# Attention scores on TensorE: four 32-row tiles in two rounds, or four 64-row tiles in one

## What is computed

```
Q = (q @ wq + bq).reshape(b, sq, H, DK).transpose(0, 2, 1, 3)
K = (k @ wk + bk).reshape(b, sk, H, DK).transpose(0, 2, 1, 3)
V = (v @ wv + bv).reshape(b, sk, H, DK).transpose(0, 2, 1, 3)
scores = jnp.einsum('bhqd,bhkd->bhqk', Q, K) / np.float32(np.sqrt(DK))
scores = jnp.where(mask[:, None, :, :] == 0, jnp.float32(-1e+20), scores)
A = jax.nn.softmax(scores, axis=-1)
out = jnp.einsum('bhqk,bhkd->bhqd', A, V).transpose(0, 2, 1, 3).reshape(b, sq, D)
out = out @ wo + bo
```

## Time and profile before

| | |
|---|---|
| median of 3 runs | 714.12 us (712.08 to 714.96) |
| the profiled execution | 715.84 us |
| its span in the profile | 714.0 us |
| busy: PE, DVE, ACT, POOL | 660.5, 510.5, 455.2, 320.0 us |
| PE L570 (scores), L607 (transposes) | 125.2, 120.3 us |
| DVE L1106 (maximum), L1122, L1065 | 108.9, 108.3, 91.8 us |
| POOL L500 (masked keys) | 95.5 us in 96 instructions |

### The profile page before, as it was taken

The page is one execution under the profiler, slowest core; times in us unless marked ns, Lnnn a source line. Parts: engine busy times, 40 slices in busy tenths (PEclk is TensorE's granted clock), DMA queues, the critical chain, the costliest instruction groups (busy, mean ns, idle before and its releaser), DMA issues.

```text
span 714.0 us, 26835 instructions
## 1 busy us (share of the span) xinstructions
PE 660.5 (92%) x9470; PEld 468.4 (66%) x9470; DVE 510.5 (71%) x1259; ACT 455.2 (64%) x1274; POOL 320.0 (45%) x540
## 2 busy tenths in 40 slices
PE   1999999999999999999999849899997899999995
PEld 1566666677777766666666536799993556666773
DVE  0599899878788778888888743344433788988884
ACT  1366777677777787777777533455524667777874
POOL 2244444467666653333377564255433345442110
PEclk9999999999999999999999769999995899999998
DMA  8333343322332310101011000122232000000100
GB/s 268 104 93 88 85 94 79 73 64 50 78 96 84 104 54 25 29 24 32 24 43 37 25 31 31 50 67 64 68 90 81 24 25 23 22 17 17 36 28 27
DMA packets 48527, 42.07 MB, mean 59 GB/s; under 512 B 6553, under 2 KB 42909, under 8 KB 47280
## 3 DMA queue, kind: packets, MB, share of 16 engines
q1 hardware_dynamic: 41632, 23.33, 11.6%
q10 hardware_dynamic: 4528, 13.25, 7.5%
q0 software_dynamic: 2272, 4.24, 1.9%
HBM read 25.41 MB, written 14.79 MB: 56 GB/s over the span
## 4 chain that ended last, share of the span: by engine, by line
PE 71%; issue 14%; POOL 7%; DVE 3%; ACT 2%; ACTq 1%; DMA 0%; SPq 0%; POOLq 0%; DVEq 0%
PE ps L570 11%; PE ps L607 10%; PE ps L738 5%; PE ps L811 5%; PE ps L800 5%; PE ps L663 5%; PE ps L644 4%; PE ps L680 4%; PE ps L746 4%; PE ps L719 3%; POOL k_by_j L500 3%; PE ps L664 2%; PE ps L766 2%; PE ps L592 2%; PE ps L691 2%
## 5 line engine op out<-in xcount | busy, mean ns | idle before, releaser
L1106 DVE TENSOR_REDUCE top<-ps 128x16 f32<-128x1024 f32 (+1 forms) x96 | 108.9, 1134 | 41.9 <-PE ps L570 40.2
L492 POOL TENSOR_TENSOR rstd<-spread,half_neg 128x1 f32<-128x1 f32 x80 | 44.5, 557 | 194.4 <-DVE spread L1199 115.2
L500 POOL TENSOR_TENSOR k_by_j<-k_t,cst 128x512 f32<-128x512 f32 (+1 forms) x96 | 95.5, 995 | 74.2 <-ACT k_t L915 37.8
L570 PE MATMUL ps<-k_by_j,q_t 32*64 32x256 f32 (+1 forms) x1536 | 125.2, 396 | 1.1
L607 PE MATMUL ps<-cst,prob 128*128 128x128 f32 x704 | 120.3, 291 | 1.1 <-ACT prob L936 1.0
L607 PEld LDWEIGHTS ps<-cst,prob 128*128 128x128 f32 x704 | 77.2, 144 | 62.0 <-issue 45.6
L1065 DVE RECIPROCAL inv<-ps 128x128 f32<-128x128 f32 x96 | 91.8, 956 | 32.3 <-PE ps L746 30.0
L1122 DVE TENSOR_TENSOR prob<-ps,top 128x1024 f32<-128x1024 f32 (+1 forms) x96 | 108.3, 1128 | 0.7
L936 ACT ACTIVATE prob<-prob 128x1024 f32<-128x1024 f32 (+1 forms) x96 | 94.8, 987 | 22.0 <-DVE prob L1122 21.7
L885 ACT ACTIVATE prob_t<-ps 128x512 f32<-128x512 f32 (+1 forms) x96 | 53.9, 561 | 38.7 <-PE ps L607 38.3
L873 ACT ACTIVATE prob_t<-ps 128x512 f32<-128x512 f32 (+1 forms) x96 | 53.9, 561 | 29.6 <-PE ps L607 28.5
(11 more groups left out here) (155 smaller groups left out, 1202.4 us busy)
## 6 DMA issues: line engine op xcount, KB each, us to landing
sorted_rows<-zero_rows ACTq DMA_DIRECT2D x32, 276.2 KB, 2.7
stage_m<-in_m SPq DMA_DIRECT2D x80, 64.0 KB, 1.9
mow<-in_mow SPq DMA_DIRECT2D x18, 256.0 KB, 3.0
stage_kv<-in_ctx_t SPq DMA_DIRECT2D x64, 64.0 KB, 1.7
rows_in<-sorted_rows SPq DMA_DIRECT2D x39, 65.0 KB, 1.8
wat<-in_wat ACTq DMA_DIRECT2D x1, 1280.0 KB, 6.5
x_t<-in_x_t SPq DMA_DIRECT2D x16, 64.0 KB, 1.9
stage_kv<-in_x_t SPq DMA_DIRECT2D x16, 64.0 KB, 1.7
```

Of the source, the lines that this page charges most:

```text
L500: pool.tensor_tensor(k_by_j[:, p, 0:nj, :], k_t[:, p:p + 1, :].broadcast_to([128, nj, TOK]), cst[:, cj:cj + nj].unsqueeze(2).broadcast_to( ...
L570: mm = pe.matmul(ps[S * b:S * b + S, 2 * p + bank, r * nj * S:(r + 1) * nj * S].rearrange("p (h k) -> p h k", k=S), q_t[rows_g, p, S * b:S ...
L1106: dve.tensor_reduce(top[:, p, 0:nh].rearrange("p (b h) -> p b h", b=2), sc, AX.X, ALU.max).then_inc(top_d, 1)
```

## The change

The scores of a pair are made in one round of four products. Each takes 64 partitions (half of the heads) and 512 columns, as a tile of 64 rows and 64 columns. For that the masked keys have 8 copies (4 with 8 heads), so L500 writes 1024 elements per partition in place of 512 (512 in place of 256 with 8 heads), and the columns of constants are wider. The semaphore between the rounds is gone, all eight transposes (four with 8 heads) stand together, and in the loops the four waits for a pair's scores stand in the slot before, between the products with the values and those of the row sums.

```
     def score_ready(pr):
         wait_pair(pe, pt1_e, pr, 2)
         if MASKED[pr.phase]:
             wait_pair(pe, mask_d, pr)
         wait_pair(pe, q_e, pr)
         wait_pair(pe, kj_d, pr)

     def score(pr):
-        p, nj = pr.p, heads(pr) // 4
+        p, nj = pr.p, heads(pr) // 2
         masked = MASKED[pr.phase]
         for bank in range(2):
-            rows_g = slice(32 * (2 * bank + r), 32 * (2 * bank + r) + 32)
+            rows_h = slice(S * bank, S * bank + S)
             for b in range(2):
                 mm = pe.matmul(
-                    ps[S * b:S * b + S, 2 * p + bank, r * nj * S:(r + 1) * nj * S].rearrange("p (h k) -> p h k", k=S),
-                    q_t[rows_g, p, S * b:S * b + S], k_by_j[rows_g, p, 0:nj, S * b:S * b + S],
-                    start=not masked and r == 0, stop=True, skip_group_check=True)
+                    ps[S * b:S * b + S, 2 * p + bank, 0:nj * S].rearrange("p (h k) -> p h k", k=S),
+                    q_t[rows_h, p, S * b:S * b + S], k_by_j[rows_h, p, 0:nj, S * b:S * b + S],
+                    start=not masked, stop=True, skip_group_check=True)
+        mm.then_inc(score_d, 1)
...
-        k_by_j = sb("k_by_j", [128, 2, 4, TOK])
+        k_by_j = sb("k_by_j", [128, 2, 8, TOK])
...
-                    p, nj = pr.p, heads(pr) // 4
-                    cj = C_J16 if nj == 4 else C_J8
+                    p, nj = pr.p, heads(pr) // 2
+                    cj = C_J16 if nj == 8 else C_J8
...
-                        scored = at(OFF_SCORE)
-                        if half == 0 and scored is not None:
-                            score_round(scored, 1).then_inc(score_d, 1)
...
+                    following = at(OFF_V)
+                    if following is not None:
+                        score_ready(following)
                     for k in range(step):
                         for g in range(4):
```

More of the change, by code:

```diff
@@ L69 @@
 BIASED = {0: 0, 1: 1, 4: 2}
-C_ID, C_J16, C_J8, C_IOTA, C_BASE = 0, 128, 132, 134, 142
-C_STEP, C_UPTO, C_BLOCK = 150, 166, 230
+C_ID, C_J16, C_J8, C_IOTA, C_BASE = 0, 128, 136, 140, 148
+C_STEP, C_UPTO, C_BLOCK = 156, 172, 236
 C_O16 = C_BLOCK + JB
@@ L264, in build @@
         neg_d, mask_d = sem("neg_d"), sem("mask_d")
-        round_d = sem("round_d")
         kj_d, rstd_d, gsc_d, res_d = (sem(k) for k in ("kj_d", "rstd_d", "gsc_d", "res_d"))
@@ L579, in slot @@
                 if pr is not None:
-                    p = pr.p
-                    wait_pair(pe, pt1_e, pr, 2)
-                    if MASKED[pr.phase]:
-                        wait_pair(pe, mask_d, pr)
-                    wait_pair(pe, q_e, pr)
-                    wait_pair(pe, kj_d, pr)
-                    score_round(pr, 0).then_inc(round_d, 1)
+                    if isinstance(pr.n, int):
+                        score_ready(pr)
+                    score(pr)
                 pr = follows(at, OFF_FY, FF)
@@ L665, in slot @@
                         .then_inc(proj_d, 1)
-                pr = at(OFF_SCORE)
-                if pr is not None and at(OFF_PV) is None:
-                    score_round(pr, 1).then_inc(score_d, 1)
                 pr = at(OFF_OUT)
@@ L1310, in constants @@
     cst[:, C_ID:C_ID + 128] = np.eye(128)
-    cst[:, C_J16:C_J16 + 4] = r[:, None] % 32 // 8 == np.arange(4)
-    cst[:, C_J8:C_J8 + 2] = r[:, None] % 32 // 16 == np.arange(2)
+    cst[:, C_J16:C_J16 + 8] = r[:, None] % S // 8 == np.arange(8)
+    cst[:, C_J8:C_J8 + 4] = r[:, None] % S // 16 == np.arange(4)
     cst[:, C_IOTA:C_IOTA + E] = np.arange(E)
```

11 lines of the change are left out of this document (7 added, 4 removed).

## The result

| | median of the runs, us | range | ratio to before [95% interval] |
|---|---|---|---|
| before | 714.54 | 712.08 to 716.69 | |
| after | 725.43 | 723.18 to 726.63 | 1.0158 [1.0122, 1.0194] |

The changed kernel is slower by 10.9 us; 726.0 was predicted. Its profiled execution is the fastest of its runs, 723.18 us, with a span of 721.4 (before: 715.84 and 714.0), so the two traces differ by only 7.4 us.

What follows compares the result with a forecast made beforehand. PE was taken as the bound (71% of the span), with a POOL–VectorE loop 0.17 us behind. LayerNorm +16.2, feed-forward +8.5, RMS -3.5, last phase -3.7, fills -3.5, router and combination -2.0 gave +12.0: 726 us, range 715 to 737.

Steps and rivals of the forecast that it cites:

- The round: Scores on PE: one round of 512 columns takes 1.01 us to the transposes; PE gains 0.25 us per 16-head slot.
- the keys' length: Masked keys on POOL (L500): 1024 elements take 1.89 us, 0.85 more than now.
- the hold: LayerNorm slots: normed on VectorE can't run beside POOL's masked keys and ends 0.08 us behind them.
- This ring: LayerNorm slots: POOL and VectorE wait on each other; the loop grows from 5.13 to 5.98 us, costing +16.2 us.
- Rival B: Masked keys on POOL cost twice the present, 2.08 us: +7.6 us, 733.7 us in all; chance 0.14.
- Rival A: VectorE gets in at a break within the longer keys instruction, so normed stays short: 704.4 us, faster; chance 0.09.
- Feed-forward slots: 15 periods with the feed-forward behind them: mean 7.9 us, 118.5 us in all against 110.08, +8.5 us.
- PE's own need, 110.08/15 - 0.25 = 7.1 us, is hidden below that: Feed-forward slots: PE needs only 7.1 us per slot, less than the 7.9 us mean set by POOL and VectorE.
- the ring over POOL: Feed-forward slots: power, longer keys, second power, then n_f take 2.95 us (before 2.28); whole slot 8.0 us.
- RMS slots: 14 slots without normed on VectorE: the longer keys fit POOL's idle time, PE's full 0.25 us each counts, -3.5 us.
- Last phase: Final stretch, 16 scores: PE is the bound and VectorE has no normed, so PE's gain counts, -3.7 us.
- Fills, router, experts: Two pipeline fills: -1.5 and -2 us from earlier scores; ten router and four combination slots: -2 us, bounds -4 and +2.

Runs made afterwards that it cites:

- The fastest kernel: Changed kernel with masked keys ahead of POOL's power where a LayerNorm follows, and the feed-forward score round between the transpose halves, against the kernel before: 696.79 us, 0.9729.

## Why the prediction was right, and where it was not

**The round, the keys' length and the hold** were right to a few hundredths: 1.02 us to the transposes (1.01 predicted), 1.90 us for 1024 elements (1.89), normed ending 0.08 us behind the keys, a period of 5.97 us (5.98), +11.3 and +5.0 us (+11.2, +5.0). This ring carries the result, and the kernel with y in PSUM shows that it is the reading of y from SBUF which holds normed. Under 1 us of the +11.3 is the clock: one of the 18 slots took 7.28 us at a mean clock of 0.77 in the first profile, and 6.21 at 0.90 in the second. Rival B's 2.08 us for the keys didn't come; nor did the estimate of 2.15 us from the Trainium skill's cycles per element (GPSIMD Engine Reference, Elementwise, side-by-side cycle accounting), against 1.90 in the trace. Rival A had assumed a break within an instruction. No run shows one. Between two instructions normed got in, and picked did not. The prediction put the 0.17 us that a round costs beside its columns down to a drain of TensorE; the measured 1.02 us fits a part that is paid once per round, but no run shows that it is a drain.

**Feed-forward slots**: the size was nearly right, +9.5 for +8.5, and the cause only half. The step "PE's own need, 110.08/15 - 0.25 = 7.1 us, is hidden below that" failed. PE's work is about that, but without its second round PE has to wait for xn_f, and the slot is 7.69 us even with short keys. Over the 15 slots the single round alone costs 3.7 us (113.8 in the kernel with short keys), long keys alone 8.5 us (118.6 in the kernel before with long keys), and both 9.5, since they lie side by side. The last two sums hold one slot of 10.1 us each. The prediction named "PE idle 0.8 us there ahead of xn_f's transpose" as a sign of the ring over POOL. It was there (0.78 us), and was no such sign: 0.69 of it stays when the keys are short. That one slot took 10.08 us instead of about 7.8, with a long wait and then half of the clock for a part of it, which no step had foreseen (below). Without it the 15 slots come to about +7.2, so that the size was so nearly right is in part luck.

**RMS slots**: -2.4 us for -3.5. The mis-sized term is PE's gain per slot. On its own stretch, first score to normed's transpose, it was even more than 0.25 us: 1.94 in place of 2.27 us. But the period shrank only from 5.21 to 5.01, because from normed's transpose to PE's output product (L674) it is now 1.31 us, 0.11 more than before. What L674 has to wait for, x_t on ScalarE, stands behind the two prob_t copies, and the first of these starts 1.77 us after the slot's first score (before: 1.35). PE and ACT of after:

```profile
330.45 1.09 PE L575 MATMUL ps<-k_by_j,q_t 64*64 64x512 f32 x8
...
333.70 0.46 PE L674 MATMUL ps<-wat,heads_t 128*128 128x128 f32 x2
...
332.22 0.60 ACT L870 ACTIVATE prob_t<-ps 128x512 f32<-128x512 f32 x1 [0.48 <-PE ps L608]
332.71 0.59 ACT L882 ACTIVATE prob_t<-ps 128x512 f32<-128x512 f32 x1
333.19 0.37 ACT L896 ACTIVATE x_t<-ps,vec 128x128 f32<-128x128 f32 x1
```

L674 starts 0.14 us after x_t's end (333.56 and 333.70), as the same product did before the change. By these lines it is the feed-forward's cause in a smaller size: the term took PE's gain as a whole without asking what ScalarE had done meanwhile. No run tests it in these slots.

**Last phase**: -2.2 us for -3.7, and not for the same reason. The slots in the second half of the stretch went from 4.01 to 3.70 us, 0.31 each and more than the 0.23 of the term. But the stretch has 13 periods and not 16, and three of them became longer: the first two by 0.16 and 0.18 us, where VectorE still has a normed that the keys hold (0.49 to 0.52 us in place of 0.34; the prediction had none there), and one in the middle by 0.32, whose cause stays open.

**Fills, router, experts.** The first fill gave -2.7 to -3.3 us for -1.5, the second about -3 for -2. Router and combination together gave -5.7 to -6.3 us, outside the bounds of -4 and +2. About 2 us of it are the clock: the last full router slot before the change ran at half of it, after the change nearly at the full one (windows of before, then of after):

```profile
401.55:409.93 8.38, 7.33 (x80) 4.93 (x81) 5.39 (x21) 4.12 (x12) 3.59 (x8) 0.50 0.05 17
...
416.83:422.97 6.14, 4.62 (x73) 3.06 (x73) 5.48 (x22) 4.12 (x12) 4.53 (x10) 0.91 0.13 39
```

The working gave these slots a maximum that waits for PE and nothing for the clock. Why the remaining gain is larger than assumed wasn't settled.

**Moved waits**: PE shows no idle time ahead of the row sums in the slots read. Putting the waits back to the slot's head in the single-round kernel wasn't tried.

So the total within 1 us of the forecast is partly luck: the LayerNorm slots, +16.3 us for the +16.2 predicted, were right, and the remaining terms missed by 1 to 4 us each, in both directions.

## What to carry to other kernels

When an engine that isn't the bound gets a longer instruction, look in the trace for operations of its neighbour that start in it and end with it: their length is the price, and it can be had back by placing the long instruction beside work that it doesn't hold (here operations that read PSUM, and the statistics). When two instructions of the bound are merged, ask what the second one covered: which other engine worked on the first one's result meanwhile, and what stands first in that engine's queue. A saving on the bound counts only once both are answered; here the change lost 1.6% as it was made, and gained 2.7% with two blocks of code in another place.

## What the runs showed of the hardware

- VectorE and POOL: these operations of VectorE, when they met an instruction of POOL, ended only behind it: normed by 0.08 to 0.09 us, the mask conversion by 0.03 to 0.09, the squares by 0.03 to 0.15, picked by 0.04, and the addition of an expert's rows (256 elements) by 0.28. With the keys in two instructions, 19 of 48 normed ended 0.08 us after the first and 25 after the second. In the router even a product over 16 elements was held, for up to 2.55 us, across the ends of two POOL copies that stood ahead of the keys. The same tensor_scalar read from PSUM (0.40 us against 0.34) wasn't held once in 48. Nor were the addition that makes y, with one operand in PSUM (0.28 us), and its statistics from SBUF (0.30), when the keys ran beside them at 102.98 us of the kernel with keys first everywhere.
- POOL's product with both inputs broadcast takes 0.61, 1.04 and 1.90 us for 256, 512 and 1024 elements, 1.67 ns an element; two of 512 back to back take 2.04 us.
- PE's clock: in the feed-forward slot at 160 us of after, PE had stood idle for 2.19 us ahead of xn_f; about a microsecond after it went on, the granted clock fell from the full level (2.4 GHz) to half (1.2 GHz) and stayed there until about 169 us. The same eight products that take 1.06 us at the full clock took 1.92:

```profile
164.77 0.30 PE L618 MATMUL ps<-cst,xn_f 128*128 128x128 f32 x1 [2.19 <-ACT xn_f L876]
...
166.64 1.92 PE L685 MATMUL ps<-x_t,ffw 128*128 128x128 f32 x8
```

From its first score to the next slot's, PE took 10.64 us here and 7.69 in the same slot with short keys. Of these 2.95 us, 1.50 are the longer wait (2.19 us against 0.69), and 1.45 came behind it, from xn_f to the next score (5.40 us against 3.95). The fastest kernel lost as much in a transition slot, after an idle time of 2.25 us (8.75 us, mean clock 0.80). In the kernel with short keys the same two places had 0.69 and 0.95 us of idle time and a clock of 1.00. The two profiles of the changed kernel show what the clock costs by itself: in the transition slot that begins near 272 us (271 in the second) both have the same wait of 1.80 us; in the first the clock stays at 1.00 and the slot takes 6.88 us, in the second it falls to a mean of 0.83 and the slot takes 7.97. So a wait of about 2 us can cost another 1.1 to 1.5 us behind it, and it need not: the same wait in the same kernel kept the clock in one execution and lost it in the other.
